# Norms folded into the weights, and for the last image the third layer's a and g kept in SBUF

## The reference

```python
sum_k = jnp.einsum('bikc,bkjc->bijc', a, b)
normalized = _layernorm(sum_k, ln2_w, ln2_b)
lin = jnp.einsum('bijc,dc->bijd', normalized, Wf)
return g * lin
```

## Time and profile before

| | us |
|---|---|
| median of 3 runs (12461.91 to 12466.63) | 12462.38 |
| profiled execution | 12463.64 |
| its span, first to last instruction | 12461.80 |
| prologue, up to the first gather | 211.10 |
| 128 steps, first gather to the last one's end | 11562.7 |
| last steps' rest, to the load of `xb` (starts 11795.78) | 22.0 |
| tail: norm, to the first context product (11823.59) | 27.8 |
| context, to the next stage's first DMA (11874.25) | 50.7 |
| depthwise and modulate, to the operands' norm (12217.84) | 343.6 |
| operands and their norm, to the first load of the triangle (12327.48) | 109.6 |
| triangle, to the first load of close (12394.75) | 67.3 |
| close, to the end of the span | 67.1 |

### The profile page before, as it was taken

One profiled execution on the slowest core, in us unless ns is written; L12 is line 12 of the kernel. 1 busy time (PEld: TensorE's weight loads), 2 busy tenths in 40 slices (PEclk: granted clock), 3 DMA queues, 4 the chain that ended last, 5 costly groups with the idle time before them and its releaser, 6 DMA issues.

```text
span 12461.8 us, 134594 instructions
## 1 busy us (share of the span) xinstructions
PE 7846.2 (63%) x46082; PEld 6368.5 (51%) x46082; DVE 5216.6 (42%) x6202; ACT 1688.1 (14%) x2917; POOL 8778.9 (70%) x9269
## 2 busy tenths in 40 slices
PE   5776667666467765554467765555457776655487
PEld 3554555555456644544456754444446754444373
DVE  3344444443444443343344444344344444344333
ACT  1001101010011112110011112210011111310025
POOL 3777777777777777777777777777777777777500
PEclk8887778777678877776677877776678887777698
...
GB/s 85 103 86 99 111 88 108 106 95 99 72 124 170 118 67 81 113 94 59 70 99 170 141 72 71 106 101 68 56 82 172 141 97 64 95 112 79 62 247 128
DMA packets 916735, 1280.87 MB, mean 103 GB/s; under 512 B 185384, under 2 KB 698088, under 8 KB 899112
## 3 DMA queue, kind: packets, MB, share of 16 engines
...
## 4 chain that ended last, share of the span: by engine, by line
POOL 68%; issue 23%; PE 3%; DVE 2%; DMA 1%; SPq 1%; ACT 1%; POOLq 0%; PEld 0%; ACTq 0%; DVEq 0%; PEldq 0%
POOL gat L451 68%; PE stage L974 2%; PE stage L877 1%; DVE srow L1417 1%; DMA gat<-table,idx 0%; DVE gat L1410 0%; PE acc L877 0%; DMA room<-b_d 0%; PEld acc L1081 0%; SPq L535 0%; POOLq L449 0%; DMA off<-offs 0%; PE pt L877 0%; PE acc L1081 0%; PE stage L929 0%
## 5 line engine op out<-in xcount | busy, mean ns | idle before, releaser
L451 POOL DMA_INDIRECT gat<-table,idx x9216 | 8754.4, 950 | 2978.2 <-issue 2801.3
L1081 PE MATMUL acc<-stt,wk 128*128 128x128 f32 (+1 forms) x30600 | 4372.0, 308 | 227.8 <-ACT stt L852 227.8
L1081 PEld LDWEIGHTS acc<-stt,wk 128*128 128x128 f32 (+1 forms) x30600 | 4221.4, 221 | 540.8 <-ACT stt L852 336.8
L1070 PE MATMUL pt<-mat,srow 128*128 128x128 f32 x2048 | 509.7, 396 | 3730.8 <-DVE srow L1417 3730.2
L1070 PEld LDWEIGHTS pt<-mat,srow 128*128 128x128 f32 x2048 | 329.3, 197 | 3934.4 <-DVE srow L1417 3924.5
L1386 DVE COPY idx<-idxn 128x18 uint32<-128x18 uint32 x512 | 97.3, 190 | 5305.8 <-DMA gat<-table,idx 5297.8
L1417 DVE TENSOR_REDUCE srow<-gat 128x576 f32<-128x2304 f32 x512 | 2081.0, 4064 | 0.3
L1410 DVE TENSOR_TENSOR gat<-gat,wtb 128x2304 f32<-128x2304 f32 x512 | 1306.1, 2551 | 62.5 <-DMA gat<-table,idx 62.5
L877 PE MATMUL stage<-room,mat 128*128 128x512 f32 (+1 forms) x1696 | 1011.1, 728 | 352.4 <-DVE room L1291 75.4
L852 ACT ACTIVATE stt<-pt 128x512 f32<-128x512 f32 x512 | 305.6, 597 | 5977.8 <-PE pt L1070 5973.4
L974 PE MATMUL stage<-room 128*128 128x128 f32 x7680 | 888.3, 278 | 22.4 <-DMA room<-toep 19.6
...
## 6 DMA issues: line engine op xcount, KB each, us to landing
gat<-table,idx POOLq DMA_INDIRECT x9216
...
toep<-in_taps SPq DMA_DIRECT2D x128, 224.0 KB
toep<-in_taps SPq DMA_DIRECT2D x128, 160.0 KB
...
```

The lines of the kernel that those rows point to most:

```text
L451: nc.gpsimd.indirect_dma_start(gat[r][:, k % K9 * G + k // K9, :], None, table[b].rearrange("(n e) -> n e", e=PAIR), bass.IndirectOffsetOn ...
L1070: ins = nc.tensor.transpose(pt[:, m, :], srow[r % 2][:, m * P:(m + 1) * P], M["ident"])
L1081: ins = nc.tensor.matmul(acc[a][:, 0:W], wk[0:kk, m, dx, block_at * C:block_at * C + P], stt[s][0:kk, m, dx:dx + W], start=start and m == ...
```

## The change

1. **Norms folded.** ACT no longer writes a normalised copy in context, modulate and operands. After the group norm DVE scales the rows of `wctx`, `wq`, the gate weights, and later `ccen`, by gn's scale (`scale`), PE multiplies the unscaled matrices by gn's shift (`fold`, one column each), and DVE adds the result to the biases. The products read `xb` itself.
2. The gates of context are stored by ACT's queue, not by SP's. For images 1 to 3 ACT makes both halves of the shift in the norms of layers 0 and 1; DVE had the upper half.
3. The first 12 tiles of the last image are loaded back, with their statistics, in the last three woven steps (`reload`); the tail loads the other four.
4. **Last image.** a is not stored: when its sigmoid is done, PE turns it, four transposes for each tile, and DVE copies it to `turned_a`, which lies where the gathers landed (pixels k on the partitions; row and channel behind them). g stays in `kept_g`, over `wk` and the end of `room`. The triangle loads b alone and takes row k of b as the stationary operand and every 64th element of `turned_a` as the moving one, so that the product comes out transposed; ACT writes it into `turned_a` over the channels it was made of. In close PE turns it back, four transposes for each tile, into the bank that the previous turn's residual is read from, and ACT copies it to SBUF. There is no s in DRAM, and close's turns are written out, not looped.
5. For all images, `lin` stays in its PSUM bank, so the variance's product waits for the previous turn's residual, `res_s`.

```diff
-BEHIND = (Stage(("context_norm",), 1, 1, NORM), Stage(("context",), 2, 4, 3), Stage(("depthwise",), 8, 1, 10),
-          Stage(("modulate",), 4, 2, 9), Stage(("operands_norm",), 1, 1, NORM), Stage(("operands",), 4, 2, 10),
+BEHIND = (Stage(("context_norm", "context_fold"), 1, 1, NORM), Stage(("context",), 2, 4, 3), Stage(("depthwise",), 8, 1, 10),
+          Stage(("modulate",), 4, 2, 9), Stage(("operands_norm", "operands_fold"), 1, 1, NORM), Stage(("operands",), 4, 2, 10),
+LAST = NB - 1
...
-    return plan + ([(Stage((), rest, 1, 1), b)] if rest else [])
+    return plan + ([(Stage(("reload",) if b == NB - 1 else (), rest, 1, 2), b)] if rest else [])
...
-        wk = sb("wk", [P, MCH, 3, 5 * C])
+        scaled = sb("scaled", [P, 2, P])
+        moved_by = sb("moved_by", [P, 3])
+        turned_a = gathered[:].rearrange("p r k e -> p (r k e)")[:, 0:H * C].rearrange("p (i c) -> p i c", c=C)
+        wk = room[:, ROOM:ROOM + N_WK].rearrange("p (m x c) -> p m x c", m=MCH, x=3)
+        kept_g = room[:, ROOM + N_WK - IMG:ROOM + N_WK]
...
+        def load_tiles(b, first, n):
+            sp.dma_start(xb[:, ds(first * TILE, n * TILE)], x2[:, ds(W + b * IMG + first * TILE, n * TILE)])\
+                .then_inc(xb_in, 16)
+
         def context_norm(b, i):
             yield 0
 
-            sp.wait_ge(x2_out, 16 * min((b + 1) * PER + 1, STEPS + 1))
-            load_xb(x2[:, W + b * IMG:W + (b + 1) * IMG])
+            if b < NB - 1:
+                sp.wait_ge(x2_out, 16 * ((b + 1) * PER + 1))
+                load_xb(x2[:, W + b * IMG:W + (b + 1) * IMG])
+            else:
+                sp.wait_ge(x2_out, 16 * (STEPS + 1))
+                load_tiles(b, 4 * EARLY, TB - 4 * EARLY)
+
+        def reload_begin(b):
+            sp.wait_ge(x2_out, 16 * (b * PER + 8 * EARLY + 1))
+
+        def reload(b, i):
+            yield 0
+            load_tiles(b, 4 * i, 4)
...
-                sp.wait_ge(gate_s, n + 2)
-                for par in range(2):
-                    sp.dma_start(planes(gated, b, t, par), half(gs[u], par, 4)).then_inc(cx_out[u], 16)
...
+                    if k == 0 and b == LAST:
+                        continue
...
-                sp.dma_start(ta[u], group(a_d, b, q)).then_inc(ab_in[u], 16)
+                if b < LAST:
+                    sp.dma_start(ta[u], group(a_d, b, q)).then_inc(ab_in[u], 16)
...
+                    if b:
+                        nc.scalar.activation(xn[C:P, ds(4 * t + TB * q + 1, 4), 1:W + 1],
+                                             xt(t + TB // 4 * q, slice(C, P)), ACT.Identity,
+                                             scale=gn[C:P, 0:1], bias=gn[C:P, 1:2])\
+                            .then_inc(upper, 1)
...
-            for u in range(flight(b)):
-                act.wait_ge(gate_p, b * TB + flight(b) * i + u + 1)
-                normalise(flight(b) * i + u, xc[u]).then_inc(cx_normed, 1)
...
+                                     bias=b_gate2[0:8, :])\
                     .then_inc(gate_s, 1)
+                act.wait_ge(gate_s, b * TB + flight(b) * i + u + 2)
+                for par in range(2):
+                    act.dma_start(planes(gated, b, flight(b) * i + u, par), half(gs[u], par, 4))\
+                        .then_inc(cx_out[u], 16)
...
+                if b == LAST:
+                    act.wait_ge(a_turned, n(u) - flight(b) + 1)
...
+                dst = kept_g[:, ds((flight(b) * i + u) * TILE, TILE)] if b == LAST else sg[u]
+                nc.scalar.activation(dst, banks[2 * u + 1], ACT.Sigmoid, bias=bg).then_inc(g_s, 1)
...
+                if b == LAST:
+                    nc.scalar.activation(turned_a[:, :, ds(QC * (flight(b) * i + u), QC)],
+                                         banks[2 * u].rearrange("p (c i) -> p i c", i=H), ACT.Copy)\
+                        .then_inc(so_s, 1)
+                    continue
...
+            if b == LAST:
+                yield 1
+                for u in range(flight(b)):
+                    act.wait_ge(a_turned, n(u) + TB + 1)
+                    act.wait_ge(c_cen_p, n(u) + 1)
+                    nc.scalar.activation(ss[u], banks[2 * u + 1], ACT.Copy).then_inc(so_s, 1)
...
+        def fold(*pairs):
+
+            def flow(b, i):
+                yield 12
+                pe.wait_ge(gn_done, norms[0])
+                for k, (m, w) in enumerate(pairs):
+                    ins = mm(PB[2][0:m, k:k + 1], w, gn[:, 1:2])
+                ins.then_inc(shift_p, 1)
+            return flow
...
-                pe.wait_ge(cx_normed, n + 1)
+                t = flight(b) * i + u
+                pe.wait_ge(gate_s, n - u + 1)
                 pe.wait_ge(ctx_s, n + 1)
-                mm(banks[2 * u], M["wctx"], xc[u]).then_inc(ctx_p, 1)
-                pe.wait_ge(gate_s, n - u + 1)
-                mm(banks[2 * u + 1][0:8, :], gw[:], xc[u]).then_inc(gate_p, 1)
+                mm(banks[2 * u], S["wctx"], xt(t)).then_inc(ctx_p, 1)
+                mm(banks[2 * u + 1][0:8, :], gws[:], xt(t)).then_inc(gate_p, 1)
...
             for u in range(flight(b)):
-                pe.wait_ge(t_normed, n(u) + 1)
                 pe.wait_ge(ab_s, 2 * n(0) + 1)
-                mm(banks[2 * u], M["ccen"], xm[u]).then_inc(t_cen_p, 1)
+                if b == LAST:
+                    pe.wait_ge(aT_s, n(u) + 1)
+                mm(banks[2 * u], S["ccen"], xt(flight(b) * i + u)).then_inc(t_cen_p, 1)
...
+            if b == LAST:
+                yield 9
+                for u in range(flight(b)):
+                    pe.wait_ge(ab_s, 2 * n(u) + 3)
+                    for q in range(4):
+                        ins = nc.tensor.transpose(banks[2 * u][:, q * P:(q + 1) * P], sa[u][:, q * W:(q + 1) * W],
+                                                  M["ident"])
+                    ins.then_inc(a_turned, 1)
+
+        def triangle_of_last(b, i):
+            yield 2
+            for u in range(flight(b)):
+                own = flight(b) * i + u
+                pe.wait_ge(ab_in[u], 32 * (b * IT if u < 2 else 0) + 16 * i + 16)
+                pe.wait_ge(so_s, b * TB + own + 1)
+                for c in range(QC):
+                    ins = mm(banks[2 * u][:, c * H:(c + 1) * H], tb[u][:, c, :],
+                             turned_a[:, :, ds(QC * own + c, 1)].rearrange("p i a -> p (i a)"))
+                ins.then_inc(prod, 1)
 
...
+            if b == LAST:
+                yield 1
+                for u in range(flight(b)):
+                    pe.wait_ge(res_s, n(0) + 1)
+                    for q in range(4):
+                        first = 8 * (flight(b) * i + u) + 2 * q
+                        ins = nc.tensor.transpose(banks[2 * u + 1][:, q * W:(q + 1) * W],
+                                                  turned_a[:, first:first + 2, :].rearrange("p r c -> p (r c)"),
+                                                  M["ident"])
+                    ins.then_inc(a_turned, 1)
             yield 2
             for u in range(flight(b)):
-                pe.wait_ge(s_in[u], 32 * (round_of(b, i, u) + 1))
+                if b == LAST:
+                    pe.wait_ge(so_s, n(u) + TB + 1 + flight(b))
+                else:
+                    pe.wait_ge(s_in[u], 32 * (round_of(b, i, u) + 1))
                 pe.wait_ge(c_y_s, n(u) + 1)
...
+        def context_fold(b, i):
+            yield 11
+            scale(S["wctx"], M["wctx"])
+            scale(S["wq"], M["wq"])
+            scale(gws[:], gw[:]).then_inc(folded, 1)
+            yield 13
+            dve.wait_ge(shift_p, 2 * b + 1)
+            tt(b_ctx2, PB[2][:, 0:1], V["b_ctx"], ALU.add)
+            tt(b_q2, PB[2][:, 1:2], V["b_q"], ALU.add)
+            tt(b_gate2[0:8, :], PB[2][0:8, 2:3], b_gate, ALU.add).then_inc(folded, 1)
+
...
-                tt(ym[u], banks[2 * u], rs[u], ALU.mult).then_inc(t_y_s, 1)
+                stt_(ym[u], banks[2 * u], b_cen, rs[u], ALU.add, ALU.mult).then_inc(t_y_s, 1)
+
+            if b == LAST:
+                yield 10
+                for u in range(flight(b)):
+                    t = flight(b) * i + u
+                    dve.wait_ge(a_turned, b * TB + t + 1)
+                    nc.vector.tensor_copy(turned_a[:, ds(8 * t, 8), :],
+                                          banks[2 * u].rearrange("p (i c) -> p i c", c=C)).then_inc(aT_s, 1)
...
-                dve.wait_ge(g_in[u], 16 * (round_of(b, i, u) + 1))
-                dve.wait_ge(res_s, n(0) + 1)
-                stt_(lin[u], banks[2 * u + 1], bf, gt[u], ALU.add, ALU.mult).then_inc(lin_s, 1)
+                if b < LAST:
+                    dve.wait_ge(g_in[u], 16 * (round_of(b, i, u) + 1))
+                t = flight(b) * i + u
+                gate = gt[u] if b < LAST else kept_g[:, t * TILE:(t + 1) * TILE]
+                stt_(banks[2 * u + 1], banks[2 * u + 1], bf, gate, ALU.add, ALU.mult).then_inc(lin_s, 1)
             yield 9
...
-                tt(res[u], lin[u], xt(flight(b) * i + u), ALU.add).then_inc(res_s, 1)
```

(1 more changed line is left out.)

115 lines of the change are left out of this document (74 added, 41 removed).

## The result

The changed kernel takes 12374.10 us, median of 4 runs (12373.78 to 12375.10), against 12462.15 for the kernel before in the same comparison (4 runs, 12461.74 to 12466.63): a ratio of 0.9928, 95% interval 0.9916 to 0.9941. The profiled execution has a span of 12373.3, 88.5 less than before.

| stretch | before | after | measured | forecast |
|---|---|---|---|---|
| prologue, to the first gather | 211.1 | 211.5 | +0.4 | 0 |
| 128 steps, to the last gather's end | 11562.7 | 11538.5 | **-24.2** | 0 |
| rest of the last steps, to the load of `xb` | 22.0 | 22.4 | +0.4 | 0 |
| norm and fold | 27.8 | 14.0 | -13.8 | -13.9 |
| context | 50.7 | 41.2 | -9.4 | -14.7 |

The account below looks back on a forecast made before the run. GpSimd's gather queue was taken to bound the 128 steps, so only the tail could gain: -14.5 + 0.6 - 14.7 - 0.5 + 0 - 8 - 37.6 + 14 = -60.7, giving 12402 us, range 12376 to 12434.

Parts of the forecast that it names:

- The failed step: In the 128 gather steps: GpSimd's queue alone bounds them, so other engines' work removed there gains 0.
- Rival C: Tail's gain eaten: slow strided triangle operand gives 12443, or ACT's doubled shift reaching GpSimd gives 12471; chance 0.09 together.
- Norm and fold: Start of the tail: loading and measuring four tiles instead of 16 gives -14.5 us, the fold +0.6.
- Context: Context stage of the tail: without gate stores on SP, PE bounds at 2.0 us a tile; -14.7 us, bounds -11 and -18.
- this wait: In context, PE's gate product waits for ACT's gate eviction only a turn later, so nothing else is late.
- Operands: Operands stage of the tail: turns stay at 23.5 us (0, bounds +6 and -5); fewer SP stores at its end give -8.
- Triangle: Last image's triangle: 67.3 us becomes 29.7, -37.6, bounds -41 and -29; three turns of 6.2 us after the first.
- Close: Last image's close: waiting for all four residuals, then transposes, and a colder PE cost +14 us, bounds +4 and +22.
- no change: Close's first turn loses its wait for s and gains the transposes; first Ln stays 10.2 us after the start.
- The sum of the tail's terms: All stage terms after the steps, from norm to close, add to -60.7 us.
- A: The better ends: turned operand at full rate, PE warm in close; triangle -41, context -18, close +4; 12383, chance 0.15.

Follow-up runs that it names:

- Runs 1 to 3: Changed kernel with VectorE's upper shift half (1) or `lin` in SBUF (2) again: 13.3 and 12.7 us back; kernel before with both edits alone (3): 22 us faster.
- run 15: Changed kernel with context's two gate stores back in SP's queue: context 51.1 us against 41.2; profiled execution 12385.91 us, three others 12404 to 12408.
- run 7: Changed kernel plus one unused VectorE reduction of 512 SBUF elements in each of 512 rows: 1.4 us more outside the depthwise steps.
- Run 8: Changed kernel with the triangle's moving operand read as 128 adjacent columns (other data), not every 64th element: 12363.68 us, ratio 0.9915; triangle 23.9 us against 32.0.
- Runs 9 and 14: Changed kernel, close's PE waiting for one tile's residual, not all four: 18603.97 us (1.0027) on a slow chip; repeated elsewhere, 616.3 us after the last gather against 623.3.
- 5 to 7: Changed kernel plus one unused VectorE instruction a row: scaling (+19.5 us in all), sum of two SBUF operands (+30.7), reduction (1.4 outside depthwise steps).

## Why the prediction was right in the tail and wrong in the steps

**The failed step** is "the 128 steps are GpSimd's queue and nothing else, and neither ACT, DVE, SP nor PE work taken out of them is worth anything". It is GpSimd's queue, but the length of a gather in it is not fixed. The term of the steps was put at 0 and measured -24.2. Runs 1 to 3 show that the two edits costed at nothing are worth 22 to 26 us, nearly the whole miss of 28; the tail gave 4.4 more than its sum. The reading that hid it: 128 equal windows have 90.3 us each by construction, whatever the steps do, and a mean of 950 ns hides a gather of 2963. GpSimd's timeline of the kernel before around 675 us shows that gather in one row. Rival C did ask whether the shift reaches GpSimd, but by ACT being late, not by VectorE being relieved; and no rival had a gain in the steps.

The Trainium skill (SBUF — State Buffer, "Who interferes with whom") says that VectorE shares one pair of SBUF ports with GpSimd, that a scaling from SBUF to SBUF can take both and a sum of two SBUF operands the shared read port, and that a reduction never contends. The runs agree in kind: outside the depthwise steps 11, 22 and 1.4 us for the three added instructions. The Trainium skill says there that whoever issues first has the pair for the whole instruction while the other is blocked; measured is more than one instruction: gathers of 2.96 and 4.81 us beside series of scalings that start every 0.47 and 0.33 us. No run looks at the ports themselves.

**Norm and fold**: right. Forecast 4.9 us from the load to the statistics, four tiles of them, and 1.8 for the fold. The trace has 4.8, 2.47 for four tiles, and 2.0 (gn ready at 11784.33, first product at 11786.37):

```profile
11772.38 0.34 SPq L543 DMA_DIRECT2D room<-x  x1
11777.20 2.47 DVE L1246 BATCH_NORM_STATS2 stats<-room 128x6 f32<-128x512 f32 x4 [6.79 <-DMA room<-x]
11784.17 0.16 DVE L1292 SCALAR_TENSOR_TENSOR gn<-stage,gn 128x1 f32<-128x1 f32 x1
11784.36 0.48 DVE L1352 TENSOR_SCALAR scaled<-mat,gn 128x128 f32<-128x128 f32 x2
11786.37 1.21 PE L926 MATMUL stage<-room,scaled 128*128 x1 [0.85 <-DVEq L425]
```

**Context**: SP was the bound before and is it again with the gates (run 15). Without them PE is, as forecast, but a tile takes 2.24 us and not 2.0, since each turn waits once for ACT's last gate eviction of the turn before: 8.1 of products and 0.86 of wait make 8.97. The prediction had this wait and held it to cost nothing. ACT's new issues don't make it: run 15, in which they are SP's, has the same 8.97 and the same 0.86 in its first turns. The first turn, with a granted clock of 0.50 up to 11792, takes 11.7 (PE's products start at 11786.37 and 11798.08). Three times 0.97 are 2.9 of the miss of 5.3; the rest is the first turn's 3.7, less 1.4 at the stage's end. -9.4 lies outside the term's bounds of -11 and -18.

**Operands**: the end went as forecast, -8.4 (last g at 12261.15, first load at 12264.50). The turns, held to stay at 23.5, take 20.93; this term was put at 0 and three turns gave -7.6, most of the -8.4 by which the stage beat its forecast. The chain behind the last g:

```profile
12239.91 1.04 PE L1092 MATMUL stage<-mat,room 128*128 128x128 f32 x8
...
12240.23 0.69 ACT L856 ACTIVATE room<-wtb,fused 128x512 f32 x1 [0.17 <-PE wtb L926]
...
12242.78 1.28 ACT L840 ACT_TABLE_LOAD   x1 [1.87 <-PE stage L926]
12244.08 1.26 ACT L840 ACTIVATE room<-stage,moved_by 128x512 f32<-128x512 f32 x2
```

The table load stands behind the wait, as read from before. The 16 transposes took 1.75 us and not 2.6 (0.44 a tile; 0.65 was the slower row), and Square follows the last g by 3.85 where it was 4.8. That is 1.0 of the 2.5 a turn. From the first Square's start to the last one's end it takes 2.42 us now (12244.08 to 12246.50) and took 4.15 before, 1.7 less. The rows of before show why: PE stood idle for ACT's normalisation, and its `ccen` products then ran at a granted clock of 0.50 (12297.70 to 12299.40), so that the Squares waited for PE:

```profile
12295.25 2.69 PE L877 MATMUL stage<-room,mat 128*128 128x512 f32 x4 [3.00 <-ACT room L686]
...
12299.68 0.60 ACT L805 ACTIVATE room<-acc 128x512 f32<-128x512 f32 x1 [1.11 <-PE acc L877]
```

In the changed kernel the transposes fill this gap, the clock is 1.00 through the `ccen` products, and the Squares stand one behind the other (0.2 us of the gain is lost again behind them). The sum had the transposes as a cost alone. This is read from the rows; no run tested it.

**Triangle**: the mechanism held and the operand's price lay at the upper bound, 1.755 us a tile against bounds of 1.06 and 1.8. That DVE's 1.76 ns an element comes so near to PE's 1.71 a column is luck as far as the runs show: the packed reduction of run 7 takes 676 ns for 512 elements, 1.32 each, so DVE's price need not be the step's. Three turns at 7.03 and not 6.2 make the 2.3 us of the miss. Run 8 shows that it is the step of the operand. By the rule of the Trainium skill that the prediction cites (SBUF — State Buffer, "Door 1: The DMA port swizzle") the product would be at the upper end or beyond it, and it lies at the upper end.

**Close**: the new wait costs what was forecast. From the last residual to the next Ln it takes 8.0 us (12313.83 to 12321.85) where it took 3.4:

```profile
12313.15 0.68 DVE L1487 TENSOR_TENSOR room<-wtb,room 128x512 f32<-128x512 f32 x1
...
12321.85 0.69 ACT L809 ACTIVATE room<-stage,eps 128x512 f32<-128x512 f32 x1 [0.26 <-PE stage L926]
```

The three gaps are 8.0, 9.2 and 7.8 us, and 3.3, 3.7 and 3.5 before; from the first turn's first Ln to the last turn's it takes 56.8 us and not 43.4, +13.4 against the forecast of +14. What was mis-sized is the first turn: "no change" became -3.5 (Ln 6.7 us after the stage's start, 12303.23, and not 10.2), as the first transposes need no load. Runs 9 and 14 show that half of the three turns' price can be had back by waiting tile by tile.

The sum of the tail's terms was thus right within 5 us, with errors of +5.3, -8.4, +2.3 and -4.3 that cancelled; that is luck. Of the rivals, A has the measured total's neighbour (12383; its terms as written add to -77, so 12385) for a reason that isn't the measured one: the operand was at its dear end, and context and close were not at their good ones.

**Open**: what starts and what ends a hold inside a longer series; why two sums back to back cost 0.26 us each and single ones 0.055; why the added instructions of 5 to 7 make depthwise's own dearer by 8 us; what makes every gather of some executions 1 to 3 ns longer, which is the 20 us by which they differ, and what makes the gathers pause on two other chips.
